# Attention one to three batches ahead of the FFN, rest-dependent products last in a group, and all engines' lists reordered, in a fused post-LN attention and FP4-FFN kernel

## The reference

```python
v = out32 @ W_write.T                       # values
# chunked scan, algebraically: reads = (x x_shifted^T * decay mask) v
return out + alpha * (reads @ W_read.T)     # _L0_attn_ref
...
def fp4_quant_dequant(x):                   # blocks of 16
    scale = jnp.maximum(jnp.max(jnp.abs(xb), axis=-1, keepdims=True) / 6.0, 1e-12)
    idx = jnp.searchsorted(_MID, jnp.abs(xb / scale))
    return _GRID[idx] * jnp.sign(xn) * scale
gate = fp4_linear(x, w_gate); y = fp4_linear(x, w_up)
h = jax.nn.silu(gate) * y
return fp4_linear(h, w_down)                # _L0_ffn_ref
...
x = _layernorm(x + _L0_attn_ref(x, ...))
x = _layernorm(x + _L0_ffn_ref(x, ...))
```

## Time and profile before

| | |
|---|---|
| median of 3 runs | 336.86 us |
| the profiled execution, device time | 338.22 us |
| its span in the trace | 336.5 us |
| PE busy | 314.3 us (93%), 2243 matmuls |
| PE weight loads busy | 305.7 us (91%) |
| DVE busy | 293.1 us (87%) |
| POOL busy | 250.7 us (74%) |
| ACT busy | 213.7 us (64%) |
| PE's part of the chain that ended last | 77% |
| DMA | 15.71 MB, mean 47 GB/s |

### The profile page before, as it was taken

One profiled execution on the slowest core, in us unless ns is written; L12 is line 12 of the kernel. 1 busy time (PEld: TensorE's weight loads), 2 busy tenths in 40 slices (PEclk: granted clock), 3 DMA queues, 4 the chain that ended last, 5 costly groups with the idle time before them and its releaser, 6 DMA issues.

```text
span 336.5 us, 6824 instructions
## 1 busy us (share of the span) xinstructions
PE 314.3 (93%) x2243; PEld 305.7 (91%) x2243; DVE 293.1 (87%) x749; ACT 213.7 (64%) x516; POOL 250.7 (74%) x261
## 2 busy tenths in 40 slices
...
DMA packets 8243, 15.71 MB, mean 47 GB/s; under 512 B 1168, under 2 KB 5264, under 8 KB 8208
## 3 DMA queue, kind: packets, MB, share of 16 engines
...
## 4 chain that ended last, share of the span: by engine, by line
PE 77%; DVE 6%; ACT 6%; POOL 5%; issue 3%; DMA 1%; ACTq 0%; POOLq 0%; DVEq 0%
PE bank L1524 12%; PE bank L1526 12%; PE bank L1525 12%; PE gu L1524 11%; PE gu L1526 10%; PE gu L1525 10%; PE bank L1598 6%; PE bank L1574 2%; DMA scal<-in_log_alpha_dram 1%; DVE h_g L989 1%; POOL wq_gu L348 1%; PE bank L1608 1%; ACT h_sq L570 1%; PE bank L1609 1%; POOL h_n L343 1%
## 5 line engine op out<-in xcount | busy, mean ns | idle before, releaser
L1524 PE MATMUL gu<-guT_hi,xqT_hi 128*128 128x352 f32 x256 | 85.2, 333 | 0.2 <-DVE xqT_lo L1076 0.2
L1526 PE MATMUL gu<-guT_hi,xqT_lo 128*128 128x352 f32 x256 | 82.5, 322 | 0.0
L1525 PE MATMUL gu<-guT_lo,xqT_hi 128*128 128x352 f32 x256 | 82.5, 322 | 0.0
L397 POOL TENSOR_TENSOR h_q<-h_g,h_ns 128x704 f32<-128x704 f32 x32 | 45.4, 1420 | 18.9 <-DVE h_g L989 18.8
L1524 PEld LDWEIGHTS gu<-guT_hi,xqT_hi 128*128 128x128 f32 x256 | 48.1, 188 | 1.0 <-DVE xqT_lo L1076 0.5
L1525 PEld LDWEIGHTS gu<-guT_lo,xqT_hi 128*128 128x128 f32 x256 | 48.2, 188 | 0.2
L1526 PEld LDWEIGHTS gu<-guT_hi,xqT_lo 128*128 128x128 f32 x256 | 48.1, 188 | 0.0
L390 POOL TENSOR_TENSOR h_n<-w_raw,h_rs 128x704 f32<-128x704 f32 x32 | 46.1, 1442 | 2.5 <-DVE h_rs L979 2.4
L643 ACT ACTIVATE w_raw<-gu 128x352 f32<-128x352 f32 x64 | 29.5, 461 | 28.4 <-PE gu L1526 28.0
L1526 PE MATMUL bank<-dnT_hi,hqT_lo 128*128 128x256 f32 x160 | 44.7, 280 | 0.0
L1525 PE MATMUL bank<-dnT_lo,hqT_hi 128*128 128x256 f32 x160 | 44.7, 279 | 0.0
...
## 6 DMA issues: line engine op xcount, KB each, us to landing
...
scal<-in_decay_dram ACTq DMA_DIRECT2D x1, 0.5 KB, 3.1
scal<-in_log_alpha_dram ACTq DMA_DIRECT2D x1, 0.5 KB, 5.0
```

The lines of the kernel that those rows point to most:

```text
L397: nc.gpsimd.tensor_tensor(blocks(h_q[:, p, 0:I]), blocks(h_g[:, p, :]), per_block(h_ns[:, p, :], HB), ALU.mult).then_inc(h_quant, 1)
L1524: nc.tensor.matmul(dst, lh, rh, start=(first and i == 0), stop=False)
L1525: nc.tensor.matmul(dst, lh, rl, start=False, stop=False)
L1526: last = nc.tensor.matmul(dst, ll, rh, start=False, stop=(i == len(terms) - 1))
```

## The change

- x1 has four buffers (`XBUF`) instead of two. The residual is written straight into x1 and normalised in place; z is gone. `x_layernorm` no longer waits for old output residuals; `x_residual` waits for them instead (`o_ready`), four batches back. z_off and o_off, outputs that nobody reads, are BF16.
- Every product group on PE is split: the matmuls that need only hi (and rests already there) come first, then a wait for the rest, then the others. `split_matmuls` puts lo·hi last; the new `late_matmuls` (scores, reads) puts both rest products last. The head of a group now waits for the hi semaphore only.
- The PSUM tables are new. All lists are reordered: attention runs up to three batches ahead of the FFN, and the body runs for b = 2, 3, 4 instead of 2 to 5. The number of each kind of operation is the same.

```diff
-        z = sb("z", [P, TILES, D])
-        z_off = sb("z_off", [P, TILES, D])
+        z_off = sb("z_off", [P, TILES, D], BF16)
-        x1 = sb("x1", [P, 2, TILES, D])
+        x1 = sb("x1", [P, XBUF, TILES, D])
...
-        v_bank, xq_bank = (bank[2], bank[1]), (bank[1], bank[2])
-        s_bank, r_bank = (bank[1], bank[3], bank[3], bank[3]), (bank[2], bank[0])
+        v_bank, xq_bank = (bank[2], bank[1]), (bank[0], bank[2])
+        s_bank, r_bank = (bank[1], bank[3], bank[0], bank[3]), (bank[2], bank[3])
...
             def x_rstd(n, u):
                 pool.wait_ge(z_var, 2 * n + u + 1)
+                if n > 0:
+                    pool.wait_ge(x1_ready, 2 * n + u - 1)
...
-            def x_layernorm(n, par, u, reused=True):
-                if reused:
-                    act.wait_ge(o_ready, 4 * n - 6 + 2 * u)
+            def x_layernorm(n, u):
                 act.wait_ge(z_shift_ready, 2 * n + u + 1)
+                z = x1[:, n % XBUF, :, :]
...
             def x_residual(n, u, reused=True):
-                    dve.wait_ge(x1_ready, 2 * n + u - 1)
+                    dve.wait_ge(z_var, 2 * n + u - 1)
+                if n >= XBUF:
+                    dve.wait_ge(o_ready, TILES * (n - XBUF) + 2 * u + 2)
+                z = x1[:, n % XBUF, :, :]
...
-            def split_matmuls(dst, terms, first=True):
+            def split_matmuls(dst, terms, rests, first=True, end=True):
                 for i, (lh, ll, rh, rl) in enumerate(terms):
                     nc.tensor.matmul(dst, lh, rh, start=(first and i == 0), stop=False)
                     nc.tensor.matmul(dst, lh, rl, start=False, stop=False)
-                    last = nc.tensor.matmul(dst, ll, rh, start=False, stop=(i == len(terms) - 1))
+                wait_all(rests)
+                for i, (lh, ll, rh, rl) in enumerate(terms):
+                    last = nc.tensor.matmul(dst, ll, rh, start=False, stop=(end and i == len(terms) - 1))
                 return last
+            def late_matmuls(dst, terms, rests):
+                for i, (lh, ll, rh, rl) in enumerate(terms):
+                    nc.tensor.matmul(dst, lh, rh, start=(i == 0), stop=False)
+                wait_all(rests)
+                for i, (lh, ll, rh, rl) in enumerate(terms):
+                    nc.tensor.matmul(dst, lh, rl, start=False, stop=False)
+                    last = nc.tensor.matmul(dst, ll, rh, start=False, stop=(i == len(terms) - 1))
+                return last
...
             def scores(n, j, free):
-                pe.wait_ge(xT_lo_ready, 2 * n + 2)
+                pe.wait_ge(xT_hi_ready, 2 * n + 2)
...
             def down(k, t, free):
-                pe.wait_ge(hT_lo_ready, 2 * k + 2)
+                pe.wait_ge(hT_hi_ready, 2 * k + 2)
...
 # PE's list, head
             scores(0, 1, [])
-            w_transpose(0, [])
-            w_transpose(1, [])
+            scores(0, 2, [])
...
 # PE's list, tail
+            gate_up(31, 7, 3, 1)
+            down(26, 2, [(o_ready, 25)])
             h_transpose(28, 0, 0, [(o_ready, 26)])
-            gate_up(31, 7, 3, 1)
```

More of the change, by code:

```diff
@@ L234, in run @@
         def run(body):
-            for b in range(2, B - 2):
-                body(b, b % 2)
+            for b in range(2, 5):
+                body(b)
         block = ctx.enter_context(nc.Block())
@@ L1702, in _ @@
[L1702 to L1723 removed]
+            reads(2, 1, [(wT_lo_ready, 8)])
@@ new lines, in _ @@
+            xq_transpose(1, 0, [(wT_lo_ready, 7)])
+            h_transpose(0, 0, 0, [(pr_ready, 13)])
+            values(3, 0, [(wT_lo_ready, 9)])
+            h_transpose(0, 0, 1, [(xqT_lo_ready, 3)])
+            gate_up(4, 1, 0, 0)
+            scores(3, 1, [(z_ready, 6)])
+            gate_up(4, 1, 0, 1)
+            pe.wait_ge(wT_lo_ready, FILLS)
+            down(0, 0, [(pr_ready, 14)])
+            h_transpose(1, 1, 0, [(hT_lo_ready, 1)])
+            scores(3, 2, [(hT_lo_ready, 2)])
+            gate_up(5, 1, 1, 0)
@@ new lines, in _ @@
+            reads(3, 0, [(v_lo_ready, 7)])
+            h_transpose(1, 1, 1, [(pr_ready, 15)])
+            gate_up(5, 1, 1, 1)
+            down(1, 1, [(hT_lo_ready, 3)])
+            xq_transpose(1, 1, [(z_ready, 7)])
+            h_transpose(2, 2, 0, [(hT_lo_ready, 4)])
+            values(3, 1, [(o_ready, 2)])
+            scores(3, 3, [(o_ready, 1)])
+            gate_up(6, 1, 2, 0)
+            h_transpose(2, 2, 1, [(xqT_lo_ready, 4)])
+            h_transpose(3, 3, 0, [(hT_lo_ready, 5)])
@@ new lines, in body @@
+                reads(n + 1, 0, [(v_lo_ready, 2 * n + 3)])
+                down(k - 4, 0, [(pr_ready, k + 10)])
+                xq_transpose(n - 1, 1, [(z_ready, 2 * n + 3)])
+                down(k - 3, 1, [(hT_lo_ready, 2 * k - 5)])
+                gate_up(k + 1, b, 1, 1)
+                h_transpose(k - 2, 2, 0, [(hT_lo_ready, 2 * k - 4)])
+                scores(n + 1, 3, [(o_ready, 4 * n - 7)])
+                values(n + 1, 1, [(o_ready, 4 * n - 6)])
+                h_transpose(k - 2, 2, 1, [(xqT_lo_ready, 2 * n)])
@@ new lines, in body @@
+                gate_up(k + 2, b, 2, 0)
+                h_transpose(k - 1, 3, 0, [(hT_lo_ready, 2 * k - 3)])
+                gate_up(k + 2, b, 2, 1)
+            run(body)
+            down(14, 2, [(pr_ready, 28)])
+            scores(7, 0, [(v_lo_ready, 14)])
+            h_transpose(15, 3, 1, [(hT_lo_ready, 30)])
+            gate_up(19, 4, 3, 0)
+            scores(7, 1, [(o_ready, 15)])
+            scores(7, 2, [(hT_lo_ready, 31)])
+            gate_up(19, 4, 3, 1)
+            reads(6, 1, [(pr_ready, 30)])
```

1429 lines of the change are left out of this document (781 added, 648 removed).

## The result

| | median of 5 runs | lowest to highest |
|---|---|---|
| before | 336.81 us | 336.72 to 336.92 |
| after | 338.38 us | 337.81 to 338.81 |

The ratio is 1.0040, interval 1.0027 to 1.0053: slower by 1.6 us. Predicted was 332.5 us, in a range that ended at 336.1. The profiled execution after took 337.93 us, with a span of 336.2.

A forecast was written before the change was run, and what follows sets the result against it. PE was taken as the bound from 60 to 257 and 285 to 316.9 us, leaving head, a short gap and tail. −3.8 + 1.0 − 0.5 + 0.6 − 1.7 = −4.4 gave 332.5 us, range 330.2 to 336.1.

The forecast's parts named there:

- Sum: Whole kernel: all terms add to −4.4 us, taken against the median of 336.86, giving 332.5 us.
- the low stretch: Head before: granted clock 0.50 from 28.4 to 35.2 us, 26 matmuls, priced at 2.5 us.
- Head, −3.8: Up to the first gate/up product: gate_up(0) at 41.3, comparable 44.9 with the reads behind it, against 48.66.
- the walk: Step-by-step timing of the new order with the old durations, in the head putting gate_up(0) at 41.3 us.
- Clock, +1.0 with an end at +1.9: Head: new idle stretches may lower the clock from about 21.5; 1.0 us taken, 0 and 1.9 kept.
- Middle, −0.5: FFN stages: attention further ahead covers the FFN's chain, removing idle and small waits; bounds −1.0 and +2.0 us.
- switches, +0.6: PE: 70 switches from transposes to products against 63 before, 0.08 us each.
- Tail, −1.7, bounds −0.5 and −2.1: After gate_up(31): 9.9 us of PE work covers the 9.28 us chain, gaining 1.7 us of a possible 2.1.
- 1: Head: the x chain takes 5.1 us again instead of 2.8; gain only 2.1, 334.8 us; chance 0.24.
- 2: Product groups: 104 inside waits cost 0.08 us each, 8.3 in all, 340.8 us; 0.06 with other slower cases.
- 3: Head and later: clock falls at 21.5 and again, x chain late too; about −0.2, 336.7 us; chance 0.07.
- the second fall: After the new waits: the lower clock comes again, for a third of the 6.8 us, costing 1 us.

The follow-up runs named there:

- e12: The kernel before with 20 unread 512-column products put ahead of five waits in its head: 336.88 us, ratio 0.9997.
- e6: The changed kernel with 15 unread 512-column products put ahead of the wait for comb_lo: 336.58 us, ratio 0.9987.
- e7: The changed kernel, early DVE and ACT order put back, then DVE's head list in PE's order of need and ACT's x_deviations(0,0) ahead of w_round(2): 336.37 us.
- e16: The changed kernel with ACT's w_squares(0) ahead of x_round(0,0) and DVE's both w_magic_add ahead of w_to_grid(0): 338.09 us, ratio 1.0028.
- e17: The changed kernel with w_maxima(4) behind w_to_grid(2) and rest_comb ahead of w_divisors(3): 337.56 us, ratio 1.0022.
- e13: e7 with two DVE moves behind the head, h_rest(2,2,0) ahead of x_moments(3,0) and h_rest(21,1,1) ahead of h_maxima(25,1): 335.70 us.
- e15: The changed kernel with the unread products of e6 and the two DVE moves of e13: 335.61 us, ratio 0.9962.
- e1: The kernel before with only the product groups split, rest-dependent products last and waits inside: 336.64 us, ratio 0.9992.
- e5: The changed kernel with the old product groups, their waits at the head: 338.57 us, ratio 1.0055.

## Why the prediction was wrong, by its own steps

- **Sum.** The step that failed first is the sentence "The terms are differences, so against the median of 336.86". The head's term was a difference against an execution of 338.22, not against the usual one. The head gained against gate_up(0) at 48.66; in the usual execution it stands at about 47.4 (e12). 1.3 us of the −3.8 was nothing, and the 1.4 us between the profiled time and the median should have said so. The 2.5 us that I had for the low stretch (26 × 0.095) was too much as well: without it gate_up(0) came 1.3 us earlier.
- **Head, −3.8.** At full clock gate_up(0) came at 42.75 (e6), and with the 3.6 us of reads behind it, which is priced and not measured, that compares as 46.4 with 47.4: −1.1. Of the −3.8, 1.3 went with the baseline; the rest, 1.4, is the walk's 41.3 that was 42.7. There I priced PE's products and took DVE's times for granted. comb_lo was put at 20.6 and came at 21.9; v_lo and the decay products stood behind weight work on DVE (e7 gives 0.3 of it back at full clock).
- **Clock, +1.0 with an end at +1.9.** The mechanism was right, and so was the place: a fall at 21.5 was feared, to 26.6 at worst; 20.9 to 27.7 was measured. The size was at the bad end, 1.8 (e6 against after), and all five executions had a mean clock of 0.988 or less. The walk had two idle stretches of 1.4 us; there was one of 3.7, because the scores ran at a spacing of 0.23 (15.63 to 15.86), not at the 0.43 that I carried over, and so were done at 18.2 instead of 19.2, and comb_lo was later.
- **The skill's rule that I set aside.** I wrote that three runs within 0.16 us don't bear out that the point where the clock changes varies from run to run (the Trainium skill, TensorE: Matmul & The Clock Gate, "Part 1: The HAM clock gate", which says it of the rise behind a kernel's first matmuls). For the head of this kernel the runs bear out that the clock varies between executions of one kernel: twelve of 117 of before at 0.988, five of them 1.4 us longer, and 2.6 us between the executions of e16 and of e17. Three runs could not show it, but the fourth, the profiled one, did: it lay 1.3 us outside them.
- **Middle, −0.5, and switches, +0.6.** The sign of the first was wrong. From gate_up(0) to gate_up(31) the kernel before takes 261.8 us (e12), 265.4 with the 3.6 of reads that the change puts behind gate_up(0); the changed kernel takes 266.5. So the two terms together are +1.1, where +0.1 was predicted. 0.7 to 1.0 of it (e13 against e7, e15 against e6) is two waits of a transpose for a bank that the new table gives to neighbouring tiles. I had counted PE's work between steps and never asked which banks the transposes share. Switches weren't measured by themselves; little is left for them.
- **Tail, −1.7, bounds −0.5 and −2.1.** The sign was right and the size far too large: −0.4 to −0.5 by the traces (20.1 us from gate_up(31) on, where before took 20.5 and 20.6). The walk took all waits away and kept the chain at 9.28 us. The wait at 319.88 was answered by one of 0.62 at 320.03, for the remainder of h(28), and h_transpose(31) still waited 0.29 for POOL's h_q at 326.00, 11.35 us behind gate_up(31), which ends at 314.65.
- **Rivals.** 1: not seen, the x chain was faster than walked. 2: refuted by e1 and e5. 3, which had 0.07, is the nearest: the fall at 21.5 was there, the second fall and rival 1 weren't; the middle took their place.

Sum as measured, against the usual execution of before: head −1.1, clock +1.8, middle and switches +1.1, tail −0.4, in all +1.4, against +1.6. The 3.6 us of reads stand in two of these terms with opposite signs and cancel. The 0.2 that is left is not assigned. Between this sum and the predicted −4.4 lie 2.7 us in the head, 0.8 in the clock, 1.0 in the middle and 1.3 in the tail: the head's is the largest, and all erred to the same side.
